# A fifth second-layer tile per batch computed from two halves in a two-layer graph network kernel, with the subtractions at other steps and two loads of x moved

## What is computed

```python
h = jnp.einsum('bnf,fo->bno', input, W)
e = h @ a1 + jnp.swapaxes(h @ a2, 1, 2)
e = jnp.where(e >= 0, e, 0.2 * e)
attention = jax.nn.softmax(adj * e, axis=1)
x = jnp.einsum('bij,bjo->bio', attention, h) + bias[None] + input
...
support = jnp.einsum('bnd,df->bnf', x, W) + b
y = jnp.einsum('bnm,bmf->bnf', adj, support)
mean, var = over batches and nodes
out = relu((y - mean) * rsqrt(var + 1e-5) * gamma + beta) + x
```

## Time and profile before

| | |
|---|---|
| runs, median (lowest to highest) | 900.86 us (900.61 to 905.04) |
| the profiled execution, and its span | 902.67 us, 900.9 us |
| PE, matmuls | 858.1 us busy, 95% |
| ACT | 809.5 us, 90% |
| DVE | 777.9 us, 86% |
| POOL | 200.5 us, 22% |
| moved by DMA | 288.35 MB, 319 GB/s from and to HBM |

### The profile page before, as it was taken

One profiled execution on the slowest core, in us unless ns is written; L12 is line 12 of the kernel. 1 busy time (PEld: TensorE's weight loads), 2 busy tenths in 40 slices (PEclk: granted clock), 3 DMA queues, 4 the chain that ended last, 5 costly groups with the idle time before them and its releaser, 6 DMA issues.

```text
span 900.9 us, 9248 instructions
## 1 busy us (share of the span) xinstructions
PE 858.1 (95%) x3271; PEld 567.3 (63%) x3271; DVE 777.9 (86%) x846; ACT 809.5 (90%) x640; POOL 200.5 (22%) x168
## 2 busy tenths in 40 slices
PE   7999999999999999999999999999999999999960
PEld 5334666675666766676666766676666666666850
DVE  3664878989898989989898999989899898999966
ACT  5998789989998999999999899989999899998745
POOL 0102022203251133303331032501333033310000
PEclk9999999999999999999999999999999999999995
DMA  8998589888888789897998889897888978886988
GB/s 333 422 381 283 187 314 346 321 299 309 355 342 292 278 342 350 320 348 254 359 359 294 299 307 355 324 324 267 349 345 320 339 247 359 313 258 212 424 330 345
DMA packets 48525, 288.35 MB, mean 320 GB/s; under 512 B 5816, under 2 KB 6440, under 8 KB 15712
## 3 DMA queue, kind: packets, MB, share of 16 engines
q1 hardware_dynamic: 43584, 252.11, 72.9%
q0 software_dynamic: 4896, 35.65, 13.0%
HBM read 263.51 MB, written 24.23 MB: 319 GB/s over the span
## 4 chain that ended last, share of the span: by engine, by line
PE 79%; DMA 8%; ACT 6%; DVE 3%; issue 1%; SPq 1%; DVEq 0%; ACTq 0%
PE acc L576 31%; PE acc L545 9%; PE acc L549 9%; PE acc L543 9%; DMA adj_slot<-adjT 5%; PE acc L530 4%; PE acc L557 3%; ACT hi L706 3%; PE acc L504 3%; PE acc L590 2%; PE acc L592 2%; PE acc L595 2%; DMA adj_slot<-xT 2%; DVE scores L828 2%; PE acc L605 1%; PE acc L608 1%
## 5 line engine op out<-in xcount | busy, mean ns | idle before, releaser
L828 DVE CUSTOM_DVE_ANT_0 scores<-scores,adj_slot 128x2048 f32<-128x2048 f32 x128 | 296.7, 2318 | 59.2 <-DMA adj_slot<-adjT 30.5
L685 ACT ACTIVATE scores<-adj_slot,f_cols 128x2048 f32<-128x2048 f32 x128 | 255.4, 2002 | 17.4 <-PE acc L549 13.1
L864 DVE SCALAR_TENSOR_TENSOR exp_lo<-scores,rz,hi 128x2048 fp32r<-128x2048 f32 (+1 forms) x133 | 266.8, 2024 | 0.0
L692 ACT ACTIVATE scores<-scores,neg_mx 128x2048 f32<-128x2048 f32 x128 | 255.2, 1994 | 11.9 <-DVE neg_mx L831 11.9
L706 ACT ACTIVATE hi<-scores,rz 128x2048 fp32r<-128x2048 f32 (+1 forms) x133 | 227.9, 1733 | 20.3 <-DVE rz L840 20.2
L576 PE MATMUL acc<-adj_slot,region_even 128*128 128x512 f32 x400 | 178.9, 592 | 0.0
L576 PE MATMUL acc<-adj_slot,region_odd 128*128 128x512 f32 x296 | 132.6, 592 | 0.8 <-issue 0.8
L576 PEld LDWEIGHTS acc<-adj_slot,region_even 128*128 128x128 f32 x400 | 75.4, 189 | 77.5 <-issue 74.2
L549 PE MATMUL acc<-exp_lo,h_hi 128*128 128x512 f32 x448 | 120.4, 390 | 0.0
L545 PE MATMUL acc<-hi,h_hi 128*128 128x512 f32 x448 | 119.9, 389 | 0.0
L549 PEld LDWEIGHTS acc<-exp_lo,h_hi 128*128 128x128 f32 x448 | 83.5, 188 | 19.0 <-DVE exp_lo L864 1.9
(11 more groups left out here) (91 smaller groups left out, 800.7 us busy)
## 6 DMA issues: line engine op xcount, KB each, us to landing
adj_slot<-adjT SPq DMA_DIRECT2D x173, 1024.0 KB, 6.8
adj_lo<-adjT POOLq DMA_DIRECT2D x26, 1024.0 KB, 5.9
adj_slot<-xT SPq DMA_DIRECT2D x20, 1024.0 KB, 8.9
adj_slot<-biasT POOLq DMA_DIRECT2D x8, 1024.0 KB, 11.8
xp_dram<-adj_slot SPq DMA_DIRECT2D x32, 256.0 KB, 6.8
adj_slot<-xp_dram SPq DMA_DIRECT2D x8, 1024.0 KB, 12.2
adj_slot<-f_rows SPq DMA_DIRECT2D x7, 1024.0 KB, 7.3
adj_slot<-y_dram SPq DMA_DIRECT2D x7, 1024.0 KB, 12.3
```

The source lines that it names most:

```text
L685: act.activation(scores[t % ER][:, :], slots[f1_slot(bt.par)][:, :], ACT.Prelu, bias=f2_cols[:, bt.n, t:t + 1], alpha=ALPHA).then_inc(edge ...
L692: act.activation(scores[e][:, :], scores[e][:, :], ACT.Exp, bias=neg_mx[:, e:e + 1], accum_out=zsum[:, e:e + 1]).then_inc(exp_done, 1)
L828: dve.tensor_tensor_reduce(scores[e][:, :], scores[e][:, :], slots[s][:, :], 1.0, NEG_BIG, ALU.mult, ALU.max, mx[:, e:e + 1]).then_inc(max ...
L864: dve.scalar_tensor_tensor(exp_lo[e][:, part_cols(t, i)], scores[e][:, part_cols(t, i)], rz[:, e:e + 1], hi[m][:, part_cols(t, i)].bitcast ...
```

## The change

Tile number 12 of the second layer is done in halves too, in the six batches that had four such tiles; the first batch has two as before, now 12 and 14 instead of 10 and 14. The high half of number 12 is loaded by POOL between the fourth and fifth `split_h` of a batch step, into the slot that number 7 used, and the tile that belongs into that slot is loaded again after number 12 instead of 7. The subtractions for 3, 7, 10, 12 and 14 stand in steps 1, 5, 7, 9 and 11 (before: 1, 5, 8 and 11 for 3, 7, 10 and 14). T_X and T_RES change places (slots of tiles 10 and 11), which moves `load_residual` from after number 12 to after number 11 and `load_x_for_h` from after number 12 to after number 13. In batch step 0 `load_residual` is issued right behind the stores of f_rows.

```diff
-    T_F, T_HI, T_X, T_RES = 8, 9, 10, 11
+    T_F, T_HI, T_RES, T_X = 8, 9, 10, 11
...
-    HI_AT = {3: T_F, 7: 2, 10: 3, 14: T_HI}
-    LOW_STEP = {3: 1, 7: 5, 10: 8, 14: 11}
-    RELOAD = {T_F: 3, T_HI: 4, T_X: 5, T_RES: 6}
+    HI_AT = {3: T_F, 7: 2, 10: 3, 12: 2, 14: T_HI}
+    LOW_STEP = {3: 1, 7: 5, 10: 7, 12: 9, 14: 11}
+    RELOAD = {T_F: 3, T_HI: 4, T_RES: 5, T_X: 6}
...
-    FIRST_HI = [10, 14]
+    FIRST_HI = [12, 14]
...
                     for c in range(NC):
                         sp.dma_start(f_rows[:, cols(c)], f_sb[QF * c:QF * c + NF, :]).then_inc(f_stored, 16)
+                    load_residual(bt)
                     sp.wait_ge(f_stored, 16 * NC)
...
                     load_f1(nx)
-                    load_residual(bt)
...
                     split_h(bt, 3)
+                    halves_of(pv, 12, load_hi)
                     split_h(bt, 4)
```

## The result

| | before | after |
|---|---|---|
| median, us | 901.64 (900.61 to 905.04, 4 runs) | 925.53 (923.77 to 925.99, 3 runs) |
| ratio to before, 95% | | 1.0248 [1.0218, 1.0277] |
| profiled execution, us (its span) | 902.67 (900.9) | 925.99 (924.2) |

The changed kernel is slower by 2.5%, 24 us. (A fourth run of it, at 2998.83 us, was disturbed and is left out of every figure.) The forecast of 904, with a range to 911, was wrong, and no rival held it.

The account below looks back on a forecast made before the run. Each batch step's tail was taken as a tie between PE's work and the chain over load, DVE and ACT. ACT's wait net of PE's gain, +7.3 us, and batch step 0, -4.1, gave 904 against the median 900.86; range 894 to 911.

Parts of the forecast that it names:

- the part on transfers: Six more 1 MB loads from POOL, moved loads of x and moved reload: cost and gain zero.
- Cost and gain zero, with that cover: Loads of x leave the place ahead of tile 15's load; no net effect, as ACT and DVE are late anyway.
- that load should then be nearer 7 us than 8.4: Tile 15's load gets shorter, worth up to 1 us a step if ACT and DVE were not late.
- ACT's wait for part_hi: ACT's casts wait for numbers 10 and 12, some 2.7 and 0.6 us; hi(14) 1.3 us late, batch step 3 105.5 us.
- its high end: PE stalls in two tiles for exp_low by 1 us each, delaying number 13 and tile 15's load; batch step 107 us.
- the sum had 91.0: In batch step 3 DVE comes to tile 15's score at 390.4, where it stood before, with nothing left.
- rival D: DVE is the bound: exp_low late, PE stalls, number 13 and tile 15's load later; 908.9 us, chance 0.23.
- PE's gain of 0.67 us a tile: A halved tile saves PE 0.67 us, 4.0 us over batch steps 2 to 7, if PE is the bound.
- Batch step 0: Earlier load of x and bias shrink PE's idle 2.67 us, clock stays at 2.4 GHz: -4.1 us, bounds 0 and -4.5.
- DVE without a wait for the load before tile 15's score: Sign expected in the trace after: DVE not idle for the load ahead of scoring tile 15.
- batch steps of 105 to 106: Sign expected in the trace after, in us; the forecast is wrong if batch steps are at 104 or less.
- the rivals: PE stays bound, 892.8 us (0.10); slack just enough, 896.8 (0.24); DVE bounds, 908.9 (0.23); the forecast itself 0.43.

Follow-up runs that it names:

- e6: Kernel before with only the second load of tile 2 moved from after number 7 to after number 12; 916.73 us against 903.53, ratio 1.0142.
- e5: Changed kernel with the second load of tile 2 after number 15 instead of after number 12; 912.59 us, ratio 1.0101.
- e1: Kernel before with only the two loads of x exchanged (T_X and T_RES, RELOAD with them); 902.94 us, ratio 1.0007.
- e7: Changed kernel with POOL's bias transfer held until DVE has scored tile 15; 912.87 us, ratio 1.0112.
- e4: Changed kernel with part_high on ACT behind exp_high in its step instead of ahead of edge; 927.02 us, ratio 1.026.
- e10: Changed kernel with tile 2's reload after number 15, bias held until tile 15 is scored, part_high behind exp_high on ACT; 909.16 us, ratio 1.0091.
- e3: Kernel before with only load_residual of batch step 0 moved right behind the stores of f_rows; 899.25 us, ratio 0.9958.
- e9: Changed kernel with tile 2's second load after number 15 and the bias transfer held until tile 15 is scored; 918.93 us, ratio 1.0205.
- e12: Kernel before with batch step 0's load_residual moved, bias held until tile 15 is scored, and a fifth halved tile at number 5; 898.43 us, ratio 0.9952.
- e8: Changed kernel with load_x_for_h one number later, after number 14 instead of right behind tile 15's load; 924.84 us, ratio 1.0232.

## Why the prediction was wrong, point by point

- **The step that failed** is in the part on transfers: "Cost and gain zero, with that cover. The reload after number 12 instead of 7 is needed only in the next batch step: zero." I priced the moved reload by when its data are wanted, and not by what it stands ahead of. It stands one place ahead of the load of tile 15, with which the tail of each batch step begins. e6 measured that alone: +13 us. Taking it out again (e5) gives 13 of the 24 back.
- **"that load should then be nearer 7 us than 8.4"** was the opposite of what came: 11.6. The two loads of x leave the place ahead of it, as said, and moving them alone does no harm (e1: 0). But load_residual goes out one number earlier (373.97), so POOL can issue the bias ahead of tile 15's load instead of behind it. With the reload there as well, the transfers run without a pause into the bias. e7 measured the bias's part: again 13 us. The two gains are not a sum: removing either is enough to take the load (nearly) out of the chain, and then ACT is next. The bias was in no term of the forecast.
- The Trainium skill, page "DMA: Bandwidth & Descriptors", section "Issuing engines are not separate DMA queues", says that transfers started by different engines run on the same 16 DMA engines and interleave. The trace agrees: POOL's bias slows SP's load, and holding POOL's took SP's load out of the chain (e7). That rule stood against the change, and was not weighed.
- **ACT's wait for part_hi**: right in place and size (2.90 and 0.74 against 2.7 and 0.6), and there in batch steps 2 to 7. What it costs is seen in e7, where no load is in the tail: batch steps of 106.0, forecast 105.5. The 0.5 more is there by the cast for number 14: it starts 77.47 us into the batch step, forecast 76.98 (376.4 less 299.42), and hi(14) at 95.35, forecast 94.9. In the changed kernel itself the wait is what sends the load out 0.54 us late, by the stall for exp_low that the forecast had in its high end only; taking it away gives nothing there, since the loads take longer instead (e4).
- **DVE**: it comes to the score of tile 15 91.8 us into the batch step, where the sum had 91.0 and before it was ready at 88.8; on the way, behind the late casts, it waits 0.32, 0.97 and 0.67 us for ACT. The two subtractions for number 12 take 3.14 us (367.68 to 370.82), where I had taken 2.94 from the row for number 10; those for numbers 10 and 14 take 2.40 now. The page "VectorE: DVE Perf Modes" of the Trainium skill (section on the TRN2 errata), by which the first of the two is 2.29, fits number 14 (2.29) and not number 12 (2.48). It changed nothing. Of rival D the path is there (exp_low late, PE stalls, number 13 and the load later), at 0.54 us a batch step; its cause is not, since the path starts at ACT's wait, and in the tail DVE waits for the load.
- **PE's gain of 0.67 us a tile** never shows in the time: in no version with the tile at number 12 was PE the bound in the tail. Even with the reload, the bias and ACT's cast moved (e10) the kernel is 0.9% slower than before.
- **Batch step 0**: right, in sign, size and mechanism; -4.1 forecast, -3.8 measured by itself (e3), the gap gone and make_support at 3.84 us.
- **The sum in place of the forecast's**, from PE's rows (L504 and L557) in both traces. Batch step 0 ends, at L557, at 88.83 instead of 91.14: -2.3. Batch step 1 takes 193.80 - 88.83 = 104.97 us from there, against 194.89 - 91.14 = 103.75: +1.2, and since make_support is 1.6 us shorter in it, the rest of it is 2.9 longer, with a load of 10.30 us in place of 7.47. Steps 2 to 6 take 738.50 - 193.80 = 544.70 against 718.43 - 194.89 = 523.54: +21.2, forecast +4.0. Step 7 takes 106.49 against 103.25: +3.2, forecast +2.2. Together +23.3, which is the difference of the spans. So all of the error is in batch steps 1 to 7, where the load ends the tail.
- **The signs**: ACT's wait came, and in batch step 0 the bias at 79.8 and a clock of 1.00 in 88 to 96. "DVE without a wait for the load before tile 15's score" did not come (3.82 us), nor batch steps of 105 to 106 (108.8 to 109.1).
- **The range**: no case for a longer load of tile 15 was among the rivals, though the chain of before had that load in the tail of batch steps 1 to 6. The transfers had no bounds from rows; the spread of this load in the kernel before, 7.43 to 8.42 us, would at least have opened the range upwards by 1 us a step.

What stays open: why the reload and the bias together cost the load more than their sum, whether the store of y explains all of e9, and why the tile gives nothing at number 5 (e12).

## What to carry to other kernels

Price a transfer that is moved by its new neighbours first, and only then by when its data are wanted: find the load with which the tail of a loop begins, and see what will be in flight when it is issued, from every queue. A tie between load, DVE, ACT and PE means that a gain on one of them alone is lost, while a loss on one of them can count in full in every round, as the load's did here (18.5 of the 21.2 us of five batch steps). And read tables that set an order for what else hangs on them: here an entry for a borrowed buffer also moved the reload of that buffer.

## What the runs showed of the hardware that was not expected

- While an accumulating transfer of 1 MB (bias) and a plain load of 1 MB were under way together (386 to 392 us in the change), the DMA engines showed a share of 0.8 to 1.2 but moved only 193 to 270 GB/s, where a window of the same share without the bias showed 430. With the bias ahead of it the load took 11.6 to 11.8 us, with the bias held 4.8 to 7.7 (e7). The bias alone is not enough: without the reload, and issued 3.5 to 4.8 us ahead of the load, it left it at 6.4 to 8.4 us in e1.
- A load issued 0.4 us behind another in the same queue took little from it (e8: 0.8 us of 11.7), while one issued 5.8 us ahead cost 1.4 to 3.3 us in each of the batch steps 2 to 6 (e6).
- Two edits that each gave 13 us gave 7 together by the medians (e9): the transfers had only been pushed on to the next store, which landed after 13.0 us or more instead of 3.3 to 3.8.
- The granted clock fell to 0.50 for two microseconds behind a stall of PE of only 2.16 us in the tail. The slower products cost nothing there, since PE had to wait for ACT's last chunk of hi(15) in any case.
